# Moving the residual evictions of a graph kernel's prep stage from VectorE to ScalarE

## Chip, cores and metric

One core of a Trainium2 chip. The metric is the device time of one execution in microseconds (us), as the median of several runs. PE is TensorE, PEld its weight loads, DVE is VectorE, ACT is ScalarE, POOL is GpSimd, SP is SyncE.

## The reference

6250 nodes with 256 features each and 200,000 edges sorted by destination. After a layer norm come two graph convolutions with a residual product, then a mixture of six experts of which two are used per node. What matters here, cut down:

```
edge_index = stack([src, dst]); xn = layernorm(x)
deg = segment_sum(ones, dst); dis = rsqrt(deg); norm = dis[src] * dis[dst]
for l in range(2):
    h   = xn @ W[l]
    agg = segment_sum(norm[:, None] * h[src], dst) + b[l]
    xn  = relu(agg + xn @ resW + resb)
x = x + xn
x = x + experts(layernorm(x))          # router, top 2 of 6
```

## The kernel before

Nodes stand in 49 tiles of 128. Layer 1 and layer 2 do not gather: they multiply the 49 tiles of messages (`parts`, a float16 high part and a float16 rest per node) by matrices of edge counts (`counts`), which PE builds from one-hot rows.
The prep stage has these strands:

- **Heads and starts.** The destinations (`dst_sb`) give a histogram of every eighth edge. DVE builds one-hot rows in seven steps (`head_onehots(0)` to `(6)`), PE sums them (`count_heads`), DVE takes them out (`offsets`), PE adds over partitions just ahead of the residual product of tile `OFFSETS_BEFORE`, and DVE makes the start of each node's edges (`starts`).
- **Fetches.** POOL then issues 49 indirect DMAs, one per tile, that read 64 packed edges for each node from DRAM into `windows` (the store `packed_edges` holds source and destination in one 32-bit word, made by `pack`). Ten tiles make a batch. `key_step(n, 0..5)` on DVE waits for batch n and makes its keys and degrees, PE turns them (`turn_keys`), ACT copies them out (`keys_copy`), ACT takes the root of the degrees (`roots`), DVE makes the scale of the messages (`scale`).
- **Residual stage**, one pass over the 49 tiles. DVE takes mean and variance of a group of tiles (`stats(g)`, groups of 4, 4, 4, 6, 6, 6, 6, 6 and 7 tiles). ACT subtracts the mean (`centre`), PE transposes (`turn`), ACT copies out (`turned_copy`), PE multiplies by the residual weights (`residual` of PE, into four banks in turn, so that tile t waits for the eviction of tile t-4), and DVE scales by `rstd`, adds `bias_sum` and writes `res_rows` (`residual` of DVE, L1099). SP stores them in seven pieces.
- **Message stage**, a second pass over the 49 tiles. PE multiplies by the layer's weights (`message`), ACT writes the high part (`high`, L920), DVE the difference (`rest_of`, L1106), ACT converts it (`middle`, L924); tile t waits for the difference of tile t-3. From tile 25 on PE also builds the first pair's edge counts (`count_run`), which ACT evicts (`quad_copy`, L929), from one-hot rows that DVE builds (`pair_heads`, `pair_tiles` at the tiles `ONEHOTS_AFTER_H`).

`norms`, `disorders`, `overflow` and `flag_and_bounds` are bounds and tests that DVE fits in between. The numbers `HIST_BEFORE`, `OFFSETS_BEFORE`, `KEYS_AFTER_RES`, `KEYS_AFTER_H`, `ONEHOTS_AFTER_H` and the tests on `t` in DVE's program are the places of these steps, counted in tiles. After prep, layer 1 (`count_and_sum`) runs over 25 pairs of tiles; `add_res` there adds the residual rows, read back from DRAM into `res_tile`.

Of the kernel before, what the change touches and what calls it, by code (L numbers as in the profile page):

```python
# [18 lines left out]
P = 128  # L19
# [3 lines left out]
I32 = mybir.dt.int32  # L23
ALU = mybir.AluOpType
# [39 lines left out]
class NodeUpdate:  # L64
# [6 lines left out]
    def __init__(self, nc, l, last, sb, sem, shapes, tables, scales, both_w, bias_sum, ident, turn_bank, product_bank, router=None, carve=None):  # L71
# [14 lines left out]
        self.res_back = [sem(f"res_back{l}_{o}") for o in range(2)]  # L86
        self.sum_ready = sem(f"sum_ready{l}")
# [36 lines left out]

    def add_res(self, dve, T, o, u, tile=None):
# [4 lines left out]
        dve.wait_ge(self.res_back[o], u * 16 + 16)  # L130
# [349 lines left out]
def gnn_moe_kernel(nc, x, src, dst, gnn_w, gnn_b, res_w, res_b, router_w1, router_b1, router_w2, router_b2,  # L480
# [35 lines left out]
    with ctx:  # L516
# [152 lines left out]
        BATCH = 10  # L669
# [80 lines left out]
        squares_ready = sem("squares_ready")  # L750
        disorder_ready = sem("disorder_ready")
# [10 lines left out]
        HIST_BEFORE = (None, 1, 2, 3, 4, 5, 6)  # L762
        OFFSETS_BEFORE = 8
        NORMS_BEFORE = 20
        STATS_AFTER = (16, 20, 25, 31)

        KEYS_AFTER_RES = (29, 39)
        KEYS_AFTER_H = (9, 17, 27)
        FLAG_AFTER_H = 33
# [8 lines left out]
        ROOTS = [("rows", g) for g in range(8)] + [("nodes", 0), ("rows", 8)] + [("nodes", n) for n in range(1, batches)]  # L778
# [18 lines left out]
        ONEHOTS_AFTER_H = (6, 14, 16, 24, 27, 30, 33, 36)  # L797
# [4 lines left out]
        with nc.Block() as block:  # L802
# [39 lines left out]
            def _(pool):  # L842
# [11 lines left out]
                nc.gpsimd.tensor_scalar(node_base[:, :], node[:, :], float(P), None, ALU.mult).then_inc(consts_made, 1)  # L854
# [35 lines left out]
            def _(act):  # L890
# [41 lines left out]

                act.wait_ge(cleared, 4)
# [4 lines left out]
                for t in range(tiles):  # L938
# [6 lines left out]
                    turned_copy(t)  # L945
                    if t == 16:
# [3 lines left out]
                    if t == 36:  # L950
                        roots(0)
                    if t == 46:
                        roots(1)
# [3 lines left out]
                for t in range(tiles):  # L957
# [7 lines left out]
                    if t in (9, 17, 27):  # L965
                        roots(2 + (9, 17, 27).index(t))
# [93 lines left out]
            def _(dve):  # L1060
# [31 lines left out]

                def residual(t):
                    if t == GROUPS[group_of(t)][0]:
                        a, b = GROUPS[group_of(t)]
                        dve.wait_ge(roots_ready, ROOTS.index(("rows", group_of(t))) + 1)
                        link(nc.vector.reciprocal(rstd[:, a:b], rstd[:, a:b]))
# [11 lines left out]
                def key_step(n, step):  # L1109
# [18 lines left out]
                    if step == 3:  # L1128
                        link(nc.vector.tensor_scalar(edge_hi[:, :, :], windows[:, ts, :], 14, None, ALU.logical_shift_right))
# [37 lines left out]

                def pack():
                    dve.wait_ge(src_loaded, 16 * 4)
                    link(nc.vector.tensor_scalar(key_i[:, :], dst_sb[:, 0:cols], 14, None, ALU.logical_shift_left))  # L1170
                    nc.vector.tensor_tensor(src_sb[:, :], src_sb[:, :], key_i[:, :], ALU.bitwise_or).then_inc(packed_ready, 1)
                    dve.wait_ge(packed_ready, 1)
# [59 lines left out]
                stats(1)  # L1232
                head_onehots(2)
                head_onehots(3)
                dve.wait_ge(res_w_loaded, 16 * 3)
                for l in range(layers):
                    link(nc.vector.tensor_tensor(bias_sum[:, l, :], bias_sum[:, l, :], res_bias[:, :], ALU.add))
                head_onehots(4)
                residual(0)
                residual(1)  # L1240
                head_onehots(5)
                residual(2)
                pack()
                head_onehots(6)
                residual(3)
                stats(2)
                offsets()
                residual(4)
                residual(5)
                starts()  # L1250
                stats(3)
                for t in range(6, 13):
                    residual(t)
                stats(4)
                for t in range(13, 16):
                    residual(t)
                for t in range(16, tiles):
                    residual(t)
                    if t in STATS_AFTER:
                        stats(5 + STATS_AFTER.index(t))  # L1260
                    if t == 18:
                        disorders()
                    if t == 21:
                        norms()
                    if 24 <= t < 30:
                        key_step(0, t - 24)
                    if 34 <= t < 40:
                        key_step(1, t - 34)
                    if t == 40:
                        scale(0)  # L1270
                scale(1)
                for t in range(tiles):
                    rest_of(t)
                    if t < 6:
                        key_step(2, t)
                    if 8 <= t < 14:
                        key_step(3, t - 8)
# [1487 lines left out]
```

## Time and profile before

| | before |
|---|---|
| median of 3 runs | 1842.45 us (1842.28 to 1843.29) |
| the profiled execution's own time | 1860.24 us |
| its span, first to last instruction | 1857.5 us |
| busy PE, DVE, ACT, POOL | 1779.8, 1036.7, 802.6, 340.4 us |
| mean granted TensorE clock | 0.989 of full speed |

A row of the timeline gives start, duration, engine, line, operation, what it writes and reads, how many instructions it merges, and in brackets the idle time of its engine just before it with what ended that. A row of the table of windows gives, for one stretch, its length, the busy time of PE, PEld, DVE, ACT and POOL with their instructions, then the granted clock as a share of 2.4 GHz, the DMA engines' share and GB/s. A row of the groups of instructions gives busy time, mean ns of one, idle time before them.

### The profile page before, as it was taken

The numbers are of one execution on the slowest core, as the hardware profiler recorded it, in microseconds if no ns is written. First come the engines' busy times: TensorE is split into PE (matmuls) and PEld (weight loads), VectorE is DVE, ScalarE is ACT, GpSimd is POOL, SyncE is SP. The second block draws the span as 40 slices with busy tenths as digits, with TensorE's granted clock in tenths as the row PEclk, the third lists the DMA queues.
The fourth block names the chain that finished last, engine by engine and source line by source line (L and its number), as shares of the span: only waits on it lengthen the run. The fifth ranks groups of instructions, "written<-read, shape, count | busy, mean of one in ns | idle before, by whom it ended". The sixth has DMA issues, their size and how long they took to land. (4 is left out here: it accounts for less than half of the span.)

```text
span 1857.5 us, 41227 instructions
## 1 busy us (share of the span) xinstructions
PE 1779.8 (96%) x14272; PEld 1044.8 (56%) x14272; DVE 1036.7 (56%) x2813; ACT 802.6 (43%) x1822; POOL 340.4 (18%) x345
## 2 busy tenths in 40 slices
PE   4897999999999999999899999999999999899997
PEld 3675444444444444444444444444444478788886
DVE  7885655555555556555324444444444568555554
ACT  2467555555555555555312222222222232565553
POOL 1780000000000000000001111111111123333333
PEclk9999999999999999999999999999999999999999
DMA  7374999999898988899985555555554489323542
GB/s 222 102 133 63 334 291 319 313 319 265 269 299 260 308 249 281 318 359 337 352 318 185 184 184 184 187 186 184 184 184 184 182 261 331 94 88 112 140 135 78
DMA packets 135987, 416.81 MB, mean 224 GB/s; under 512 B 13685, under 2 KB 81611, under 8 KB 129640
## 3 DMA queue, kind: packets, MB, share of 16 engines
q1 hardware_dynamic: 90376, 255.13, 39.9%
q0 software_dynamic: 45392, 160.65, 29.6%
q8 instruction: 36, 0.59, 0.1%
q14 instruction: 39, 0.32, 0.1%
q10 hardware_dynamic: 144, 0.13, 0.0%
HBM read 162.27 MB, written 262.07 MB: 228 GB/s over the span
## 5 line engine op out<-in xcount | busy, mean ns | idle before, releaser
L1475 PE MATMUL bank<-parts,counts 128*128 128x512 f16 x4704 | 1078.9, 380 | 3.3 <-DVE counts L1590 3.3
L1475 PEld LDWEIGHTS bank<-parts,counts 128*128 128x128 f16 x4704 | 442.8, 98 | 509.0 <-issue 28.5
L1634 ACT ACTIVATE counts<-bank 128x392 f16<-128x392 f32 x768 | 336.5, 501 | 296.1 <-PE bank L631 296.1
L640 DVE TENSOR_TENSOR rows<-rows,iota_lo 128x2048 bf16<-128x2048 bf16 (+1 forms) x384 | 322.1, 890 | 20.3 <-PE bank L631 19.3
L631 PEld LDWEIGHTS bank<-rows 64*128 64x128 bf16 x6144 | 95.2, 94 | 82.1 <-issue 78.0
L467 POOL DMA_INDIRECT first_rows<-route_rows,route_spot_i x49 | 47.8, 976 | 498.7 <-DVE tokens L458 394.4
L2265 PE MATMUL bank<-y_t,counts 128*128 128x256 f32 x480 | 115.2, 383 | 5.7 <-ACT y_t L2337 5.1
L631 PE MATMUL bank<-rows 64*128 64x49 bf16 x6144 | 116.8, 185 | 0.1
L2265 PE MATMUL bank<-h_t,counts 128*128 128x256 f32 x480 | 113.7, 380 | 0.0
L2294 PE MATMUL bank<-counts,h_t 128*128 128x256 f32 x480 | 113.5, 380 | 0.0
L1490 ACT ACTIVATE middle<-bank 128x256 f32<-128x256 f32 x98 | 37.3, 381 | 175.9 <-PE bank L1475 161.7
L2479 DVE TENSOR_SCALAR h_t<-bank,counts 128x256 f32<-128x256 f32 x120 | 57.8, 482 | 89.8 <-PE bank L2265 89.8
L2265 PEld LDWEIGHTS bank<-y_t,counts 128*128 128x128 f32 x480 | 92.0, 192 | 19.2 <-issue 6.4
L2341 ACT ACTIVATE h_t<-bank,counts 128x256 f32<-128x256 f32 x120 | 56.1, 468 | 100.5 <-PE bank L2265 88.8
L2294 PEld LDWEIGHTS bank<-counts,h_t 128*128 128x128 f32 x480 | 90.8, 190 | 12.2
L2366 ACT ACTIVATE counts<-parts 128x514 f32 x135 | 92.6, 700 | 9.2 <-issue 2.3
L388 DVE TENSOR_TENSOR route_prob<-bank,router_b_sb 128x12 f32<-128x12 f32 (+1 forms) x25 | 4.3, 170 | 161.6 <-PE bank L378 161.6
L183 PE MATMUL bank<-both_w,rows 128*128 128x512 f32 x196 | 92.2, 593 | 0.0
L2265 PEld LDWEIGHTS bank<-h_t,counts 128*128 128x128 f32 x480 | 86.7, 190 | 9.5
L192 DVE TENSOR_TENSOR res_next<-bank,bias_sum 128x256 f32<-128x256 f32 x49 | 20.8, 425 | 120.8 <-PE bank L183 111.6
L1496 DVE TENSOR_TENSOR sums<-middle,bank 128x256 f32<-128x256 f32 x98 | 41.3, 421 | 82.3 <-ACT middle L1490 81.3
L2570 POOL DMA_INDIRECT first_out<-both_w,to_row x60 | 60.6, 1010 | 129.7 <-DVE both_w L2492 94.2
(275 smaller groups left out, 1759.1 us busy)
## 6 DMA issues: line engine op xcount, KB each, us to landing
counts_table<-counts SPq DMA_DIRECT2D x25, 3136.0 KB, 15.3
counts<-counts_table SPq DMA_DIRECT2D x24, 3136.0 KB, 12.5
first_rows<-zero_rows POOLq DMA_DIRECT2D x3, 10530.0 KB, 59.7
second_rows<-zero_rows POOLq DMA_DIRECT2D x3, 10449.0 KB, 77.0
first_out<-zero_rows POOLq DMA_DIRECT2D x3, 10368.0 KB, 54.9
res_tile<-res_table SPq DMA_DIRECT2D x98, 128.0 KB, 2.8
first_rows<-zero_rows POOLq DMA_DIRECT2D x1, 10270.0 KB, 58.7
second_rows<-zero_rows POOLq DMA_DIRECT2D x1, 10191.0 KB, 68.6
```

What stands on the lines that cost most here:

```text
L183: mm = nc.tensor.matmul(self.product_bank[:, :], self.x1_t[:, o, k * P:(k + 1) * P], self.both_w[:, self.l + 1, k, :], start=k == 0, stop= ...
L467: pool.indirect_dma_start(table, bass.IndirectOffsetOnAxis(ap=self.spot_i[:, b, c, o:o + 1], axis=0), rows[:, b, o, lo:hi], None, bounds_c ...
L631: mm = nc.tensor.matmul(out[:, u * tiles:(u + 1) * tiles], lo[rows, i, :, j], hi[rows, i, :, j], start=True, stop=True)
L640: return nc.vector.tensor_tensor(rows, k, v, ALU.is_equal)
L1475: mm = nc.tensor.matmul(acc[:, 0:2 * dim], counts[:, b, s, o * P:(o + 1) * P], parts[:, s, :], start=s == 0, stop=s == tiles - 1)
L1634: nc.scalar.activation(counts[:, b, :, quad_nodes(q)], bank[4 + q % 4][:, 0:RUN * tiles].rearrange("p (n s) -> p s n", s=tiles), ACT.Copy) ...
L2265: mm = nc.tensor.matmul(to[m][:, 0:ROWS], weights_of(k, n)[:, kf, m * P:(m + 1) * P], source[:, k % 2, kf, :], start=kf == 0, stop=kf == K ...
L2294: mm = nc.tensor.matmul(outs_bank[k % 2][:, cols_of], h2_t[:, k % 2, kf, h * P:(h + 1) * P], weights_of(k, 2)[:, kf, :], start=kf == 0, st ...
L2341: nc.scalar.activation(to[:, k % 2, 0, :], frm[0][:, 0:ROWS], ACT.Relu, bias=bias_of(k, n, 0)).then_inc(low_out, 1)
L2366: nc.scalar.activation(w[:, k % WB, part], held[:, bass.ds(e, 1), part].rearrange("p a n -> p (a n)"), ACT.Copy).then_inc(w_loaded[n][k % ...
L2479: nc.vector.tensor_scalar(to[:, k % 2, 1, :], frm[1][:, 0:ROWS], bias_of(k, n, 1), 0.0, ALU.add, ALU.max).then_inc(high_out, 1)
L2570: pool.indirect_dma_start(table, bass.IndirectOffsetOnAxis(ap=to_row[:, k % SB, h:h + 1], axis=0), result[:, k % 2, cols_of], None, bounds ...
```

## The change

Five edits to the prep stage, and one that follows from them in layer 1.

1. The residual products of tiles 0 to 39 are evicted by ACT, as a copy scaled by `rstd`, inside its loop two tiles behind `turned_copy`; DVE evicts tiles 40 to 48. The reciprocal of a group's `rstd` becomes a step of its own on DVE (`inverse`) with a semaphore (`rstd_ready`).
2. The bias is no longer added there. In layer 1 DVE adds it to `res_tile` (`add_bias`, 49 instructions of 128x256), ahead of `add_res`.
3. `pack` moves from DVE (two instructions) to ACT (one, which writes the destinations into the upper 16 bits of the source words); the destination then stands at bit 16 and not 14, so the shift and `node_base` change.
4. DVE's program of the residual stage is no longer tied to tiles: statistics, one-hots, starts, norms, disorders and the keys of batch 0 follow each other. `starts` comes after the sum ahead of tile 18, not 8.
5. Keys of batch 0 turn at tiles 44 to 48 of the residual stage, those of batches 1 to 4 at tiles 5, 15, 26 and 37 of the message stage (before: batches 0 and 1 in the residual stage, 2 to 4 at 9, 17 and 27). `overflow` goes to tile 39, `flag_and_bounds` from tile 40 to 46.

The paths for irregular graphs only share some semaphores, and this input does not take them.

```diff
-        HIST_BEFORE = (None, 1, 2, 3, 4, 5, 6)
-        OFFSETS_BEFORE = 8
+        HIST_BEFORE = (None, 1, 5, 7, 10, 14, 16)
+        OFFSETS_BEFORE = 18
+        LATE_RES = 40
-        ONEHOTS_AFTER_H = (6, 14, 16, 24, 27, 30, 33, 36)
+        ONEHOTS_AFTER_H = (7, 9, 17, 19, 27, 29, 37, 40)
...
+                def residual(t):
+                    act.wait_ge(products_ready, t + 1)
+                    act.wait_ge(rstd_ready, group_of(t) + 1)
+                    nc.scalar.activation(res_rows[:, t, :], res_bank(t)[:, 0:dim], ACT.Copy, scale=rstd[:, t:t + 1]).then_inc(res_ready, 1)
...
+                def pack():
+                    act.wait_ge(dst_loaded, 16 * 3)
+                    act.wait_ge(src_loaded, 16 * 4)
+                    nc.scalar.activation(src_sb[:, :].bitcast(U16).rearrange("p (c h) -> p c h", h=2)[:, :, 1], dst_sb[:, 0:cols], ACT.Copy).then_inc(packed_ready, 1)
...
+                    if 2 <= t < LATE_RES + 2:
+                        residual(t - 2)
+                    if t == PACK_AT:
+                        pack()
...
+                def inverse(g):
+                    a, b = GROUPS[g]
+                    dve.wait_ge(roots_ready, ROOTS.index(("rows", g)) + 1)
+                    nc.vector.reciprocal(rstd[:, a:b], rstd[:, a:b]).then_inc(rstd_ready, 1)
...
-                    nc.vector.scalar_tensor_tensor(res_rows[:, t, :], res_bank(t)[:, 0:dim], rstd[:, t:t + 1], bias_sum[:, 0, :],
-                                                   ALU.mult, ALU.add).then_inc(res_ready, 1)
+                    dve.wait_ge(res_ready, t)
+                    nc.vector.tensor_scalar(res_rows[:, t, :], res_bank(t)[:, 0:dim], rstd[:, t:t + 1], None, ALU.mult).then_inc(res_ready, 1)
...
+    def add_bias(self, dve, T, o, u):
+
+        dve.wait_ge(self.res_back[o], u * 16 + 16)
+        self.nc.vector.tensor_tensor(self.res_tile[:, o, :], self.res_tile[:, o, :], self.bias_sum[:, 0, :], ALU.add).then_inc(self.res_biased, 1)
...
                 for t in range(tiles):
                     rest_of(t)
+                    n, step = divmod(t - 1, BATCH)
+                    if 0 <= step < 6 and n + 1 < batches:
+                        key_step(n + 1, step)
+                    if t in SCALE_AFTER_H:
+                        scale(1 + SCALE_AFTER_H.index(t))
```

ACT's program in the middle of the residual stage, before. `counts<-counts,row_mean` is `centre`, `counts<-bank` is `turned_copy`:

```order
L893 ACTIVATE counts<-counts,row_mean 128x256
L903 ACTIVATE counts<-bank3 128x256
L893 ACTIVATE counts<-counts,row_mean 128x256
L903 ACTIVATE counts<-bank2 128x256
L893 ACTIVATE counts<-counts,row_mean 128x256
```

The same place now, with `parts<-bank,rstd` the residual's eviction:

```order
L908 ACTIVATE counts<-counts,row_mean 128x256
L918 ACTIVATE counts<-bank3 128x256
L923 ACTIVATE parts<-bank1,rstd 128x256
L908 ACTIVATE counts<-counts,row_mean 128x256
L918 ACTIVATE counts<-bank2 128x256
L923 ACTIVATE parts<-bank6,rstd 128x256
```

Each tile has a third ACTIVATE between the copy and the next `centre`.

DVE's program between `starts` and the middle of the residual stage, before (`parts<-bank,rstd,bias_sum` is its eviction of a residual):

```order
L1166 CAST start_i<-start 128x50
L1084 BN_STATS row_stats<-counts 128x6 x6
L1086 TENSOR_TENSOR row_sum<-row_stats 128x6
L1087 TENSOR_TENSOR row_gap<-row_stats 128x6
L1088 TENSOR_TENSOR row_var<-row_stats 128x6
L1089 TENSOR_SCALAR row_mean<-row_sum 128x6
L1090 TENSOR_TENSOR row_gap<-row_gap 128x6
L1091 SCALAR_TENSOR_TENSOR row_var<-row_gap,row_var 128x6
L1099 SCALAR_TENSOR_TENSOR parts<-bank,rstd,bias_sum 128x256 x2
L1097 RECIPROCAL rstd<-rstd 128x4
L1099 SCALAR_TENSOR_TENSOR parts<-bank,rstd,bias_sum 128x256 x4
```

and the end of that stretch now, from the last statistics on:

```order
L1123 RECIPROCAL rstd<-rstd 128x7
L1148 TENSOR_SCALAR key_i<-onehot_lo 128x640
L1149 TENSOR_SCALAR edge_hi<-onehot_lo 128x640
L1153 TENSOR_TENSOR node_keys<-edge_hi,node_base 128x640
L1155 CAST node_keys<-key_i 128x640
L1158 TENSOR_SCALAR edge_hi<-onehot_lo 128x640
L1160 TENSOR_TENSOR key_i<-edge_hi,node 128x640
L1162 COPY over<-key_i 128x10
L1163 TENSOR_REDUCE deg<-key_i 128x10
L1129 TENSOR_SCALAR parts<-bank,rstd 128x256 x3
```

No eviction of a residual stands on DVE ahead of the keys of batch 0; the first is that of tile 40.

DVE's program at the end of prep, now; `rest<-bank,message_scale,parts` is `rest_of`:

```order
L1135 SCALAR_TENSOR_TENSOR rest<-bank,message_scale,parts 128x256 x5
L1221 TENSOR_REDUCE over<-bank 128x1
L1222 TENSOR_SCALAR over<-over 128x1
L1223 CAST flag<-over 128x1
...
L1230 TENSOR_SCALAR dis_next<-dis,power 128x49
L1232 TENSOR_SCALAR dis_back<-dis,power 128x49 x2
L1135 SCALAR_TENSOR_TENSOR rest<-bank,message_scale,parts 128x256 x2
```

`flag_and_bounds` stands ahead of the last two differences; before, eight followed it.

## Rows read from the trace of the kernel before

**Rows 1.** Windows of the stages: residual, message with two halves, layer 1.

```profile
50.00:111.50 61.50, 53.19 (x259) 42.41 (x260) 51.68 (x156) 34.92 (x95) 47.05 (x47) 0.94 0.39 114
111.50:143.00 31.50, 29.63 (x161) 21.72 (x159) 30.09 (x62) 22.16 (x62) 29.24 (x43) 1.00 0.94 136
143.00:157.50 14.50, 10.59 (x130) 7.85 (x123) 9.12 (x18) 11.98 (x34) 0.00 (x0) 1.00 1.02 134
...
162.60:185.30 22.70, 16.44 (x182) 11.48 (x181) 14.00 (x39) 18.09 (x49) 0.00 (x0) 1.00 0.01 2
185.30:840.00 654.70, 654.63 (x7950) 323.24 (x7951) 387.07 (x607) 360.76 (x909) 37.43 (x11) 1.00 0.94 297
```

**Rows 2.** Groups of DVE's instructions, from 0 to 185 us.

```profile
L1099 DVE SCALAR_TENSOR_TENSOR parts<-bank,rstd,bias_sum 128x256 f32<-128x256 f32 x49 | 22.7, 481 | 8.8 <-PE bank L991 8.2
...
L1131 DVE TENSOR_TENSOR key_i<-edge_hi,node 128x640 f32<-128x640 int32 x5 | 4.1, 820 | 0.0
```

**Rows 3.** PE's timeline in the residual stage.

```profile
67.98 3.60 PE L1040 MATMUL bank<-parts,ones 128*128 128x512 f32 x8
...
72.50 1.03 PE L991 MATMUL bank<-both_w,counts 128*128 128x256 f32 x4
...
73.58 1.03 PE L991 MATMUL bank<-both_w,counts 128*128 128x256 f32 x4
...
80.62 1.86 PE L991 MATMUL bank<-both_w,counts 128*128 128x256 f32 x4 [2.54 <-DVE parts L1099]
...
111.47 9.01 PE L1002 MATMUL bank<-both_w,counts 128*128 128x256 f32 x40
```

**Rows 4.** DVE's timeline up to the starts and behind them.

```profile
21.04 2.02 DVE L640 TENSOR_TENSOR onehot_lo<-head_lo,iota_lo 128x3584 bf16<-128x3584 bf16 x1
...
23.76 2.02 DVE L640 TENSOR_TENSOR onehot_lo<-head_lo,iota_lo 128x3584 bf16<-128x3584 bf16 x1
...
49.22 0.19 DVE L1166 CAST start_i<-start 128x50 int32<-128x50 f32 x1
49.32 2.05 DVE L1084 BATCH_NORM_STATS2 row_stats<-counts 128x6 f32<-128x256 f32 x6
...
52.12 0.87 DVE L1099 SCALAR_TENSOR_TENSOR parts<-bank,rstd,bias_sum 128x256 f32<-128x256 f32 x2
```

**Rows 5.** POOL's timeline, first and last of the 49 fetches.

```profile
50.44 1.21 POOL L876 DMA_INDIRECT onehot_lo<-packed_edges,start_i  x1 [42.03 <-POOLq L873]
...
113.76 0.98 POOL L876 DMA_INDIRECT onehot_lo<-packed_edges,start_i  x1 [0.30 <-issue]
```

**Rows 6.** Groups of ACT's instructions, from 0 to 185 us.

```profile
L893 ACT ACTIVATE counts<-counts,row_mean 128x256 f32<-128x256 f32 x49 | 24.4, 501 | 32.2 <-DVE row_mean L1089 32.2
L920 ACT ACTIVATE parts<-bank,message_scale 128x256 f16<-128x256 f32 x49 | 23.0, 469 | 2.7 <-DVE message_scale L1141 2.2 <-PE bank L1002 0.4
...
L903 ACT ACTIVATE counts<-bank 128x256 f32<-128x256 f32 x49 | 18.5, 378 | 24.5 <-PE bank L983 24.4
...
L907 ACT ACTIVATE keys_t<-bank 128x256 bf16<-128x256 f32 x25 | 9.6, 384 | 4.8 <-PE bank L1012 4.8
...
L949 ACT ACTIVATE parts<-both_w 128x2048 f32<-128x2048 f32 x1 | 1.9, 1898 | 0.0
```

**Rows 7.** DVE's timeline in the message stage: tiles 0, 24, the bounds, tile 48.

```profile
113.04 0.48 DVE L1106 SCALAR_TENSOR_TENSOR rest<-bank,message_scale,parts 128x256 f32<-128x256 f32 x1 [0.50 <-ACT parts L920]
...
142.73 0.48 DVE L1106 SCALAR_TENSOR_TENSOR rest<-bank,message_scale,parts 128x256 f32<-128x256 f32 x1
...
173.19 0.15 DVE L1198 TENSOR_REDUCE over<-bank 128x1 f32<-128x3 f32 x1
...
176.76 0.88 DVE L1106 SCALAR_TENSOR_TENSOR rest<-bank,message_scale,parts 128x256 f32<-128x256 f32 x2
...
183.05 0.48 DVE L1106 SCALAR_TENSOR_TENSOR rest<-bank,message_scale,parts 128x256 f32<-128x256 f32 x1 [0.19 <-ACT parts L920]
```

**Rows 8.** PE's timeline, its longest idle time in the message stage.

```profile
159.18 1.75 PE L1002 MATMUL bank<-both_w,counts 128*128 128x256 f32 x4 [3.46 <-issue]
```

More of the change, by code:

```diff
@@ L23 @@
 I32 = mybir.dt.int32
+U16 = mybir.dt.uint16
 ALU = mybir.AluOpType
@@ L86, in __init__ @@
         self.res_back = [sem(f"res_back{l}_{o}") for o in range(2)]
+        self.res_biased = None if last else sem(f"res_biased{l}")
         self.sum_ready = sem(f"sum_ready{l}")
@@ L129, in add_res @@
         dve.wait_ge(self.sums_out, T + 1)
-        dve.wait_ge(self.res_back[o], u * 16 + 16)
+        if self.last:
+            dve.wait_ge(self.res_back[o], u * 16 + 16)
+        else:
+            dve.wait_ge(self.res_biased, T + 1)
         if later:
@@ L775, in keys_after_h @@
             return next(((n + len(KEYS_AFTER_RES)) * BATCH // 2 + t - a for n, a in enumerate(KEYS_AFTER_H) if a <= t < a + BATCH // 2), None)
-        ROOTS = [("rows", g) for g in range(8)] + [("nodes", 0), ("rows", 8)] + [("nodes", n) for n in range(1, batches)]
+        ROOTS = [("rows", g) for g in range(9)] + [("nodes", n) for n in range(batches)]
         def res_bank(t):
@@ L964, in _ @@
                         middle(t - 1)
-                    if t in (9, 17, 27):
-                        roots(2 + (9, 17, 27).index(t))
+                    if t in ROOTS_AFTER_H:
+                        roots(1 + ROOTS_AFTER_H.index(t))
                 middle(tiles - 1)
@@ L1232, in _ @@
                 stats(1)
+                inverse(0)
                 head_onehots(2)
                 head_onehots(3)
+                stats(2)
+                inverse(1)
+                head_onehots(4)
+                stats(3)
+                inverse(2)
+                head_onehots(5)
+                head_onehots(6)
+                inverse(3)
+                stats(4)
+                offsets()
+                stats(5)
+                inverse(4)
+                starts()
                 dve.wait_ge(res_w_loaded, 16 * 3)
@@ L1237, in _ @@
                     link(nc.vector.tensor_tensor(bias_sum[:, l, :], bias_sum[:, l, :], res_bias[:, :], ALU.add))
[L1238 to L1251, printed above, removed]
@@ L1252, in _ @@
-                for t in range(6, 13):
-                    residual(t)
[L1254 to L1270, printed above, removed]
@@ L1271, in _ @@
-                scale(1)
+                stats(6)
+                inverse(5)
+                stats(7)
+                inverse(6)
+                norms()
+                stats(8)
+                inverse(7)
+                disorders()
+                inverse(8)
+                for step in range(6):
+                    key_step(0, step)
+                residual(LATE_RES)
+                residual(LATE_RES + 1)
+                residual(LATE_RES + 2)
+                scale(0)
+                for t in range(LATE_RES + 3, tiles):
+                    residual(t)
@@ L1339, in _ @@
                 def _(act):
-                    act.wait_ge(degree_ready, 1)
-                    nc.scalar.activation(true_dis[:, :], degree[:, :], ACT.Sqrt, bias=1.0).then_inc(root_ready, 1)
+                    act.wait_ge(stage_done, DEGREES_MADE)
+                    nc.scalar.activation(true_dis[:, :], degree[:, :], ACT.Sqrt, bias=1.0).then_inc(stage_done, 1)
                 @block.vector
```

85 lines of the change are left out of this document (37 added, 48 removed).

## Prediction, on record before the changed kernel ran

> **What bounds the kernel now.** I read the table of windows first. Layer 1, the 654.7 us behind prep, has PE busy in 654.63 of them [rows 1]: a us that prep gives up moves the end of the kernel by a us, and nothing in layer 1 waits for anything else. So the question is only when prep ends, now at 185.3 us. The windows then split prep. In the residual stage, 50 to 111.5 us, PE is busy in 53.19 of 61.5 us and DVE in 51.68; neither is full. In the first half of the message stage DVE is busy in 30.09 of 31.5 us and bounds it. In the second half ACT is the fullest: 11.98 of 14.5 and 18.09 of 22.7 us [rows 1].
>
> The timeline of PE says why the residual stage is slow. Where nothing disturbs it, one tile starts 1.08 us after the other (72.50, 73.58) [rows 3]; 49 tiles would be 53 us. But DVE holds statistics, norms, key steps and evictions in one program, and PE waits for an eviction, 2.54 us in the row shown, after which the same four products take 1.86 us, not 1.03 [rows 3]: the clock had fallen from 2.4 towards 1.2 GHz while it stood, and 0.94 of full is the stage's mean [rows 1]. The stage begins early, but before the starts are made at 49.22 [rows 4] only 10 of the 49 tiles are through. Fetches run from 50.44 to 113.76 on POOL, 1.3 us apart [rows 5]; the message stage begins at 111.47 [rows 3], when the last batch is just being fetched, so a message stage that begins earlier needs key steps that come later in it.
>
> **The change, part by part.**
>
> *Start of the stage.* Up to 21.04 us DVE does what it did [rows 4]. Then come five more head one-hots at 2.72 us (23.76 less 21.04), statistics of one group of 4 (about 2.1 us, scaled from 2.80 for six tiles, 52.12 less 49.32) and one of 6 [rows 4], and four reciprocals, estimated at 0.2: the fourth reciprocal, for which ACT's eviction of tile 12 waits, is due at 21.04 + 13.6 + 4.9 + 0.8 = 40.3. Removed from this stretch are the two instructions of pack and six evictions. From there PE has tiles 14 to 17 to do (4.4 us), two head sums (about 1 us each), and ACT the squares of the weights (1.90 us, unchanged) [rows 6]: the sum ahead of tile 18 comes at 48.5, and the starts at 50.1, against 49.3. So the fetches are 0.9 us later, and PE stands at tile 18 where it stood at 10.
>
> *Pack on ACT.* No row has it. 1568 elements lie between 256 (0.38 us) and 2048 (1.90 us) [rows 6]; I take 1.5. It stands where ACT then waits for the statistics of group 2, due near 28, so it costs nothing; without that cover, 1.5.
>
> *Evictions on ACT.* The nearest row is L920, the same bank read with a per-partition scale: 469 ns, against 481 on DVE [rows 2, 6]. ACT's instructions overlap by about 0.1 us, so a tile costs centre 0.40, copy 0.28, eviction 0.37 to 0.40: 1.05 to 1.08, no more than PE's 1.08 [rows 3, 6]. I take PE's pace, 1.09 a tile, with the end of range 1.3 where the two loops lock. The Trainium skill, page "ScalarE: Activation LUTs", section "Rules for kernel authors", says to use VectorE and not ScalarE for mul and add, with up to about 3x per element. The rows have the two level for float32 out of PSUM (469 against 481), so the sum does not go by it; what it would do is a rival below.
>
> *Rest of the residual stage.* Tiles 18 to 21 end at 48.5 + 4.4 = 52.9. The norm products take 3.6 [rows 3]: 56.4. Then 27 tiles at 1.09, five turns of keys at 0.25: 87.1. DVE has 2.8 us of statistics against 6.5 us of PE per group and stays ahead, but reciprocals now wait for ACT's roots, and the keys of batch 0 (eight instructions, one of which takes 0.82 us [rows 2]; 4.6 us estimated, at most 6.6) follow the last of them, due near 77: eviction 40 comes near 82, just when PE's tile 44 needs its bank. I add 0.9. Messages begin at 88, not 111.47, and the first difference at 89.8, not 113.04 [rows 3, 7]: 23.2 us gained. The fetches of batch 0 are in by about 66 and hide.
>
> *First half of the message stage.* DVE bound it: 29.7 us from tile 0 to 24 [rows 7]. It had three batches of keys and three and a half one-hot steps; it now has nearly two and a half batches and four steps. I take 29.7 (28 to 31): tile 24 at 119.5. Batches 1, 2, 3 are wanted near 91, 103, 115 and are in by about 80, 93, 106; batch 4 is wanted at tile 31, near 131, its last fetch is issued at 114.6 [rows 5].
>
> *Second half.* 40.3 us from tile 24 to 48 [rows 7]. ACT, the fullest engine, gets ten copies of keys in it, not five. One is 0.38 us [rows 6], between 0.3 and 0.9 with the turn it waits for; at 0.5, 2.5 us. Key steps of batch 4 on DVE lie between differences: 0 to 4, I take 1. The bounds (173.19 to 176.76, 3.6 us) [rows 7] stood at tile 40, where PE and ACT could use some of it; at tile 46 only two high parts can hide them. 0 to 3.6 more, I take 1.6. PE stood 3.46 us with nothing that the profile shows before 159.18 [rows 8], while the DMA engines were full (1.02 share) [rows 1]. POOL's copies of the expert weights follow the fetches at the same time as now, and so fall wholly on this half; 0 to twice 3.5 us of it may come, I take half of what is there, 1.7 less. Sum: 40.3 + 2.5 + 1 + 1.6 - 1.7 = 43.7, so tile 48 at 163.2, against 183.05: 19.9 us earlier.
>
> *Layer 1.* 49 additions of about 0.43 us on DVE, which is busy in 387 of 655 us [rows 1]: 21 us of idle time used. The first waits for `res_tile` and holds DVE's one-hot rows behind it: 0.5 us. If the cover were gone in each of 24 pairs, up to 10 us; PE's idle time there is nil now, and DVE runs ahead by a step, so I take 0. Semaphores added cost nothing beside that.
>
> Together 19.9 - 0.5 = 19.4 us. Of the profiled execution, 1860.2 us with a span of 1857.5, 1841 would be left. Runs without the profile take 1842.45, 18 us less; I take off the same 19.4 and get **1823.0**. 0.2% (3.7 us) is about what a measurement can tell from no change.
>
> **Rivals.**
>
> *The loops lock* (0.18). ACT has three instructions a tile, each waiting on another engine, at 1.05 to 1.08 against PE's 1.08. At 1.25 a tile, 31 tiles are 5 us longer, and a second stop of PE like that at 159 adds 3.5: 1827 to 1834. For it: ACT was never above 0.6 busy in that stage [rows 1]. Against it: it is two tiles behind, with four banks.
>
> *The message stage gives back less* (0.13). No stop of PE, bounds and key steps hidden: 43.7 becomes 37 to 39, and 1817 to 1812.
>
> *ScalarE three times slower at this* (0.02). An eviction of 1.4 us makes a tile 2.1; 22 tiles from 18 to 39 are 22 us longer and the early ones 8: 1853. L920 speaks against it [rows 6]. This is where the rule of the Trainium skill's page "ScalarE: Activation LUTs" would lead.
>
> *Slower: PE at 1.2 GHz through the residual stage* (0.03). Before, the clock fell when PE had waited [rows 3]. If ACT feeds it in drops, a tile takes twice 1.08, and from 18 such tiles on the 19.4 us are gone; all 31 from tile 18 add 33 and give 1856. Against it: at 0.86 busy the clock was 0.94 of full [rows 1], and fewer waits should follow.
>
> *Nothing gained* (0.02): the bias additions take PE's cover in layer 1 and locked loops the rest; 1842.
>
> **How the numbers follow.** Forecast 0.62, 1823 with its own 1817 to 1828. The locked and the short case reach to 1834 and 1812; leaving out the outer edge of each, the range is 1813 to 1832. Faster: 0.62 + 0.18 + 0.13 = 0.93. Same 0.02. Slower 0.02 + 0.03 = 0.05.
>
> **What the changed profile would show.** Starts near 50; evictions by ACT near 470 ns; PE's residual tiles 1.09 apart from 56 on, at full clock; messages from 88; difference of tile 24 near 119.5 and of tile 48 near 163; first product of layer 1 near 165.5; layer 1 with PE full. Wrong would be: tiles 1.2 or more apart with PE waiting for ACT, DVE waiting for a fetch, or idle PE in layer 1 behind one-hot rows.

## The result, and the profile after

The changed kernel takes 1829.31 us (median of 4 runs, 1827.04 to 1832.29); the kernel before, on the same chip, 1842.87 us (4 runs, 1842.28 to 1846.48). The ratio is 0.991, 95% interval 0.9887 to 0.9932: about 13.5 us faster, where 19.4 were forecast. The two profiled executions stand further apart (1860.24 and 1832.29 us, spans 1857.5 and 1829.7); most of what prep does not explain of that lies at the border of layers 1 and 2, and is taken up under "Where the rest went".

The windows of the changed kernel, with the columns of [rows 1] (length, then busy time of PE, PE's weight loads, DVE, ACT and POOL, granted clock, DMA share, GB/s), cut where its stages begin:

```profile
50.00:88.00 38.00, 37.51 (x199) 30.77 (x198) 27.12 (x84) 30.01 (x88) 27.71 (x28) 1.00 0.41 121
...
111.50:143.00 31.50, 26.54 (x275) 18.74 (x273) 24.72 (x50) 24.88 (x70) 30.28 (x44) 1.00 0.76 99
143.00:157.50 14.50, 6.88 (x67) 5.14 (x66) 3.91 (x10) 5.64 (x16) 1.01 (x2) 0.69 1.03 140
157.50:170.40 12.90, 6.36 (x52) 4.07 (x51) 6.66 (x27) 6.98 (x20) 0.00 (x0) 0.76 0.31 56
170.40:812.00 641.60, 641.57 (x7771) 316.12 (x7772) 394.29 (x637) 352.47 (x888) 37.43 (x11) 1.00 0.94 305
```

The residual stage is 38 us long in place of 61.5 [rows 1], with PE busy in 37.51 of them at full clock. The part from 143 to 157.5 is the bad one: PE 6.88 us busy in 14.5, at 0.69 of its clock, with every compute engine idle more than it works and the DMA engines full. Layer 1 has PE full, as before.

PE's timeline of the changed kernel (start, duration, engine, line, operation, and in brackets the idle time before it and what ended it), which answers to [rows 3, 8]:

```profile
53.45 3.60 PE L1067 MATMUL bank<-parts,ones 128*128 128x512 f32 x8
...
72.06 1.03 PE L1018 MATMUL bank<-both_w,counts 128*128 128x256 f32 x4
...
73.14 1.03 PE L1018 MATMUL bank<-both_w,counts 128*128 128x256 f32 x4
...
81.39 1.10 PE L1018 MATMUL bank<-both_w,counts 128*128 128x256 f32 x4 [0.49 <-DVE parts L1129]
...
87.64 2.54 PE L1029 MATMUL bank<-both_w,counts 128*128 128x256 f32 x11
...
153.37 1.44 PE L1029 MATMUL bank<-both_w,counts 128*128 128x256 f32 x3 [6.68 <-issue]
...
170.43 5.30 PE L1489 MATMUL bank<-parts,counts 128*128 128x512 f16 x12 [6.28 <-DVE counts L1604]
```

Residual tiles start 1.08 us apart, and from 50 us on PE's only wait in that stage is 0.49 us, for DVE's eviction of a late tile. Messages begin at 87.64 (111.47 before). The next thing that stands out is 6.68 us before 153.37 that nothing in the profile ends: "issue" means that the engine waited for no semaphore that the trace shows. In what follows such an idle time is called PE's stop. Before, such a stop was 3.46 us long [rows 8].

DVE's timeline and groups of the changed kernel, against [rows 4, 7]:

```profile
50.79 0.19 DVE L1195 CAST start_i<-start 128x50 int32<-128x50 f32 x1
...
89.22 0.48 DVE L1135 SCALAR_TENSOR_TENSOR rest<-bank,message_scale,parts 128x256 f32<-128x256 f32 x1 [1.10 <-ACT parts L940]
...
118.30 0.48 DVE L1135 SCALAR_TENSOR_TENSOR rest<-bank,message_scale,parts 128x256 f32<-128x256 f32 x1
...
156.71 0.48 DVE L1135 SCALAR_TENSOR_TENSOR rest<-bank,message_scale,parts 128x256 f32<-128x256 f32 x1 [7.58 <-ACT parts L940]
...
164.22 0.15 DVE L1221 TENSOR_REDUCE over<-bank 128x1 f32<-128x3 f32 x1
...
167.78 0.88 DVE L1135 SCALAR_TENSOR_TENSOR rest<-bank,message_scale,parts 128x256 f32<-128x256 f32 x2
170.08 0.29 DVE L1604 TENSOR_TENSOR counts<-counts,ident_h 128x256 f16<-128x256 f16 x1 [1.43 <-PEq L817]
```

Tile 0's difference is at 89.22, tile 24's at 118.30: 29.1 us for the first half, 29.7 before. From tile 24 to tile 48 (the second of the two at 167.78) it is 49.9 us, where 40.3 were taken before and 43.7 were forecast. The bounds stand from 164.22 to 167.78. The groups of ACT's instructions up to 170 us (count, then busy time and mean ns) show its new work:

```profile
L940 ACT ACTIVATE parts<-bank,message_scale 128x256 f16<-128x256 f32 x49 | 23.1, 471 | 1.5 <-PE bank L1029 1.2
...
L923 ACT ACTIVATE parts<-bank,rstd 128x256 f32<-128x256 f32 x40 | 19.1, 477 | 0.8 <-DVE rstd L1123 0.8
...
L956 ACT ACTIVATE src_sb<-dst_sb 128x1568 uint16<-128x1568 int32 x1 | 2.0, 2006 | 0.0
```

### The profile page after: what moved, and what is told of

Same layout as the page of the kernel before. It is cut to its first block and busy times, and to the rows that moved or that the text cites. A ratio compares the mean times of both kernels' runs of the same rounds, so it can differ in the third digit from the quotient of the medians.

```text
span 1829.7 us, 41310 instructions
## 1 busy us (share of the span) xinstructions
PE 1769.5 (97%) x14272; PEld 1041.2 (57%) x14272; DVE 1034.7 (57%) x2820; ACT 817.5 (45%) x1863; POOL 341.2 (19%) x345
## 3 DMA queue, kind: packets, MB, share of 16 engines
q1 hardware_dynamic: 90376, 255.13, 40.3%
q0 software_dynamic: 45392, 160.65, 29.1%
```

## Experiments

Each kernel was timed in five rounds beside the kernel before. There were three groups; the kernels of one group ran on one chip, and one is compared with another only inside its group. In all of them the ratio is to the kernel before.

### First group: what holds the second half back

**The changed kernel with the copies of the expert weights in layer 1.** POOL's copies (`router_w...`, `expert_pack`), issued behind the fetches until 143.5 us, are moved to the head of `store_zeros`, ahead of the zero stores:

```diff
                 for t in range(tiles):
                     pool.indirect_dma_start(windows[:, t, :], ...)
-                pool.dma_start(router_w1_sb[:, :, :], ...)
-                for e in range(experts): ...
...
         def store_zeros(pool):
+            pool.dma_start(router_w1_sb[:, :, :], ...)
+            for e in range(experts): ...
```

> The changed kernel with POOL's copies of the router and expert weights moved out of prep, to the head of POOL's program in layer 1. Theory (PE's program load waits behind full DMA engines): the one stop of 6.7 us at 146.7 is gone, with the slow clock behind it some 8 to 10 us of prep; prep ends near 161 and the time falls from 1829 to 1819 to 1822, with less spread between runs. Rival (the stop belongs to PE's own program at that place, whatever the DMA engines do): a stop of several us stays and the time stays at 1827 to 1832. Second rival (the copies only move): the zero stores end about 30 us later and layer 2's first scatters wait, which gives part back.

Measured: 1847.75 us, ratio 1.0007 (0.9993 to 1.0021). In its trace the stop is gone and prep ends early. PE's and DVE's timeline:

```profile
160.56 0.88 DVE L1124 SCALAR_TENSOR_TENSOR rest<-bank,message_scale,parts 128x256 f32<-128x256 f32 x2
```

```profile
163.21 5.29 PE L1478 MATMUL bank<-parts,counts 128*128 128x512 f16 x12 [6.28 <-DVE counts L1606]
```

and its window, with no DMA traffic to speak of where the changed kernel had a share of 1.03:

```profile
145.00:150.00 5.00, 4.06 (x44) 3.10 (x45) 2.39 (x5) 3.44 (x11) 0.00 (x0) 0.79 0.01 3
```

Tile 24 is at 118.11 here and tile 48 at 161.0: 42.9 us without a stop, against 49.9 with one of 6.68. So the stop is nearly the whole difference, and it comes with the full DMA engines. (The granted clock falls here too, to 0.79 in the row shown, although PE did not stop.) But the 7.2 us that prep gives up are more than lost. Layer 1 is 7.9 us longer (163.21 to 909.86, against 170.43 to 909.15), and layer 2 with what follows 15.2 us (935.7 against 920.5). The zero stores start behind the copies, and the last is issued at 901.95 in place of 844.62. This is the second rival of the expectation; the 1819 to 1822 us of its theory were missed, though the stop went as it said.

**The same move in the kernel before.** 

> The kernel before with the same move of the copies. Theory: its stop of 3.5 us at 155.7 is gone, with the slow clock 4 to 5 us; 1837 to 1839. The difference between this kernel and the changed one with the same move is then what the change is worth without stops: 17 to 20 us. Rival: nothing changes, 1842, and the difference is the same 13.5 us as between the two originals.

Measured: 1869.07 us, ratio 1.0132 (1.0112 to 1.0151). Prep ends 5.7 us earlier (its first product of layer 1 at 179.6), and the kernel is 23 us slower. Both the 1837 to 1839 us of the theory and the 1842 of its rival were missed: in both kernels, moving the copies into layer 1 costs more than it gives.

**The flag and the bounds at tile 43 in place of 46.**

```diff
-                    if t == 46:
+                    if t == 43:
                         flag_and_bounds()
```

> The changed kernel with the bounds and the flag at tile 43 of the message stage, not 46. Theory (at 46 only two tiles are left to hide 3.6 us, and the profile shows ScalarE idle 3.2 us there): 1.5 to 3 us less, 1826.5 to 1828. Rival (PE then waits for the differences of tiles 44 and 45 as it did before at tile 40, and the place is worth nothing): within 0.5 us of 1829.

Measured: 1831.34 us, ratio 0.9918 (0.9902 to 0.9934): no gain. The trace says why, and it was not among the expectations. ACT's last instruction of prep, then DVE's first of layer 1, then PE's stop of the message stage and its first product:

```profile
163.75 0.42 ACT L944 ACTIVATE parts<-rest 128x256 f16<-128x256 f32 x1 [0.24 <-DVE rest L1135]
```

```profile
169.76 0.29 DVE L1604 TENSOR_TENSOR counts<-counts,ident_h 128x256 f16<-128x256 f16 x1 [6.05 <-PEq L817]
```

```profile
149.38 0.81 PE L1029 MATMUL bank<-both_w,counts 128*128 128x256 f32 x3 [2.02 <-issue]
...
170.11 4.81 PE L1489 MATMUL bank<-parts,counts 128*128 128x512 f16 x12 [7.42 <-DVE counts L1604]
```

The chain of messages was done at 164.2, 4.9 us before the changed kernel's (168.30 + 0.81 = 169.1 for ACT's last instruction), mostly because the stop was 4.7 us shorter in this execution; yet layer 1 began at the same time. Its windows of the last us of prep:

```profile
163.00:164.00 1.00, 0.00 (x0) 0.00 (x0) 0.48 (x1) 0.76 (x3) 0.00 (x0) 0.50 0.27 74
164.00:165.00 1.00, 0.00 (x0) 0.00 (x0) 0.00 (x0) 0.16 (x1) 0.00 (x0) 0.50 0.08 17
165.00:166.00 1.00, 0.00 (x0) 0.00 (x0) 0.00 (x0) 0.00 (x0) 0.00 (x0) 0.50 0.00 0
```

No compute engine works from 164.2 to 169.8; the DMA engines move the last bytes of the copies until just before 165. The new theory was that POOL's part of prep does not end before the copies are through, some 5 us after their last byte, and that this is a **floor** under the end of prep, near 169.5, just where the chain of messages ended too. Before, the copies ended near 163, but prep ended at 185, and the floor was out of sight.

**The evictions on ACT alone**, in the kernel before: its order of DVE's steps and its packing stay, the evictions of 40 residual tiles move to ACT and the bias into layer 1.

```diff
                     turned_copy(t)
+                    if 2 <= t < LATE_RES + 2:
+                        residual(t - 2)
...
+                        if there(i * 2 - 3):
+                            if r == 0:
+                                update.add_bias(dve, i * 2 - 3, 1, i - 2)
```

> The kernel before with only the evictions of tiles 0 to 39 on ScalarE and the bias added in layer 1; VectorE keeps its order with its steps tied to tiles, and the starts stay ahead of tile 8. Theory (the eviction is what tied PE to VectorE, but the order must follow, since VectorE now runs ahead into steps that wait for fetches while a reciprocal stands behind them): messages begin near 95 to 100 and key batches 2 to 4, wanted at tiles 0, 8 and 18, wait for their fetches until 118; prep ends 8 to 14 us earlier than before, 1829 to 1835. Rival (the eviction alone carries it, the order is worth nothing): 1827 to 1830, messages near 88. Second rival (the order carries it): 1840 to 1843.

Measured: 1835.83 us, ratio 0.9942 (0.9926 to 0.9958). In its trace messages begin at 103.26, 8.2 us earlier than before, and the first product of layer 1 comes at 179.24, although PE's stop is longer (4.95 us). The expectation had messages at 95 to 100 and 1829 to 1835 us; both were missed, by 3.3 and 0.8 us. So the evictions alone bring 8.2 of the 23.8 us by which messages begin earlier, and 6.1 of the 14.9 at prep's end; of the time, 0.58% of about 0.9%. The rest is put down, by difference, to the new order of DVE's steps and the packing, which stand on the freed DVE; no kernel has the new order alone. Note that 6.1 us of prep stand beside 9.9 us of time here (1845.71 less 1835.83): the time does not follow prep's end us for us.

### Second group: the copies earlier, and the bias

> The changed kernel itself, unchanged, as the reference on this chip for the others of this group. Both theories: 1829 us within 3, ratio 0.991.

Measured: 1849.75 us (1846.8 to 1853.06), ratio 0.9912 (0.9883 to 0.9941). This chip is about 1% slower in every kernel, and noisier. Its trace shows the floor in the changed kernel itself, and plainer than any other. ACT's last instruction of prep, DVE's first of layer 1 and PE's first product:

```profile
165.49 0.81 ACT L944 ACTIVATE parts<-rest 128x256 f16<-128x256 f32 x2 [3.17 <-DVE rest L1135]
```

```profile
172.30 0.29 DVE L1604 TENSOR_TENSOR counts<-counts,ident_h 128x256 f16<-128x256 f16 x1 [6.45 <-PEq L817]
```

```profile
172.65 5.04 PE L1489 MATMUL bank<-parts,counts 128*128 128x512 f16 x12 [11.31 <-DVE counts L1604]
```

PE's stop was only 3.11 us and the chain ended at 166.3, 2.8 us before that of the first execution, yet layer 1 began 2.2 us later than there (172.30 against 170.08). The copies ran until 167.5 here.

**Two of six experts copied ahead of the fetches**, in the time in which POOL waits for the starts:

```diff
+                pool.wait_ge(gnn_w_loaded, 16 * 3)
+                pool.dma_start(router_w1_sb[:, :, :], ...)
+                for e in range(2): ...
                 pool.wait_ge(packed_stored, 16)
                 pool.wait_ge(starts_ready, 1)
                 for t in range(tiles):
                     pool.indirect_dma_start(windows[:, t, :], ...)
-                for e in range(experts): ...
+                for e in range(2, experts): ...
```

> The changed kernel with the router's tables and two of the six experts' weights copied before GpSimd's fetches (issued from about 41 us, when the weights have landed, until about 50) in place of behind them; the other four stay behind the fetches, issued until about 133 us. Nothing is left out and nothing more lies in layer 1. Theory (the copies of six experts, which fill the DMA engines until 164 us, cost the preparation its end twice: TensorE's stop of 6.7 us at 147 and GpSimd's part of the preparation, which is not over before about 169): the DMA engines are free of copies by about 150, TensorE's stop shrinks or goes, the first product of layer 1 stands near 163.5 as it did with the copies in layer 1, and since layer 1 has no copies to carry, this gain stays: 1829.3 - 7 = 1822 us, ratio 0.987. Rival (the total is set by what layers 1 and 2 do with the transfers, not by when the preparation ends): no change, 1829. A second rival: the two early experts slow the packed edge list or the first fetches, the key batches come late, and the time is 1829 to 1833.

> The same with the flag and the bounds at tile 43 in place of 46. Theory: with the copies over early, the end of the preparation follows the chain of DVE and ScalarE again, so the 4 to 5 us by which this edit alone brought that chain forward (ScalarE done at 164.2 in place of 169.1) now count in part: the first layer-1 product at 159 to 161, 1818 to 1821 us, 2 to 4 below the kernel without it. Rival (something other than the copies held the end at 169.8 when the flag stood at 43): no difference to the kernel with early copies alone.

Measured: 1848.68 us (1840.6 to 1850.4), ratio 0.9881 (0.9849 to 0.9912), and with the flag at 43 1845.62 us (1840.55 to 1847.8), ratio 0.9887 (0.9854 to 0.992). The intervals overlap those of the changed kernel, so the times settle nothing here; the 1822 and 1818 to 1821 us of the theories were missed on a chip that is slower throughout, and so was the ratio of 0.987. The first products of layer 1 do bear on the floor. With the copies early alone, then with the flag at 43 too:

```profile
168.98 5.04 PE L1498 MATMUL bank<-parts,counts 128*128 128x512 f16 x12 [6.30 <-DVE counts L1613]
```

```profile
163.80 5.10 PE L1498 MATMUL bank<-parts,counts 128*128 128x512 f16 x12 [2.81 <-DVE counts L1613]
```

With the copies behind the fetches, a chain of messages that was done 4.9 us earlier moved this product by 0.3 us (170.43 to 170.11). With the copies over by about 151, the product comes 3.7 us before that of the changed kernel on this chip (168.98 against 172.65), and it follows the chain again: the flag at 43 moves it by 5.2 us, of which 3.1 are a shorter stop of PE (1.29 us) and at most 2.1 the edit. Both products came later than expected (163.5, and 159 to 161). The first expectation was wrong about the stop: it did not go but came earlier, 4.34 us before 137.98, still under full DMA engines:

```profile
137.98 0.28 PE L641 MATMUL bank<-src_sb,onehot_hi 64*128 64x49 bf16 x5 [4.34 <-issue]
```

**The bias left out.** 

> The changed kernel without the 49 additions of the bias to the residual rows of layer 1: this part of the computation is left out, everything else is as in the changed kernel. The prediction's term was 0 (plus 0.5 us for the first one): 1829 us within 1, since TensorE is full in layer 1. Rival (DVE's additions lie on the path of some tiles): 49 times 0.42 us, or some of it, is saved, down to 1809 us.

Measured: 1851.03 us (1845.63 to 1862.95), ratio 0.9926 (0.9897 to 0.9956), against 0.9912 with the additions. They cost nothing that can be seen on this noisy chip; the rival's 20 us are excluded.

### Third group: pack, and three experts early

> The changed kernel once more, unchanged: on this chip the reference for the two others of this group. Ratio 0.991, as in both groups before.

Measured: 1830.76 us (1827.51 to 1834.22), ratio 0.9918 (0.99 to 0.9935). Here PE's stop was 4.32 us and the chain ended at 166.7; layer 1 still began at the floor:

```profile
165.33 0.88 DVE L1135 SCALAR_TENSOR_TENSOR rest<-bank,message_scale,parts 128x256 f32<-128x256 f32 x2
169.44 0.29 DVE L1604 TENSOR_TENSOR counts<-counts,ident_h 128x256 f16<-128x256 f16 x1 [3.23 <-PEq L817]
```

**Pack back on DVE**, ahead of its third group of statistics:

```diff
                 head_onehots(3)
+                pack()
                 stats(2)
```

> The changed kernel with the packing of the keys back on VectorE (two instructions over 1568 columns, 0.97 and 1.79 us in the kernel before) ahead of its third statistics group, and off ScalarE (2.01 us). My theory: the starts come about 2.8 us later (53.6 in place of 50.8), fetches and key batches with them, and the messages still begin at 87.6 because the residual tiles on TensorE, 1.08 apart, set that; but GpSimd's copies end 2.8 us later too, so the floor that they put under the end of the preparation goes from about 170 to 172.5 in the profile: plus 0 to 2.5 us on the time. Rival (the preparation ends by the chain of messages alone and the copies are no floor): 0. Rival two (VectorE's delay reaches ScalarE's evictions by the reciprocals, TensorE waits, and everything moves by 2.8): plus 2.8 or more.

Measured: 1833.49 us (1831.77 to 1833.87), ratio 0.9932 (0.9915 to 0.9949), 2.7 us above the control with ranges that overlap. Its trace shows what the second rival said of the start of the messages, against my theory. Messages, PE's stop and the first product of layer 1:

```profile
91.10 1.25 PE L1027 MATMUL bank<-both_w,counts 128*128 128x256 f32 x5
...
157.37 1.44 PE L1027 MATMUL bank<-both_w,counts 128*128 128x256 f32 x3 [7.22 <-issue]
...
174.78 4.15 PE L1494 MATMUL bank<-parts,counts 128*128 128x512 f16 x12 [6.29 <-DVE counts L1609]
```

The starts came at 54.25 (51.12 in the control), and messages at 91.10 (87.97): both moved by 3.1 us, about the length of VectorE's two instructions. DVE's stretch up to the starts bounds the residual stage after all. The end of prep is 5.0 us later (174.78 against 169.79), but that is not pack's alone: the stop was 2.9 us longer in this execution, and the copies ran until 169.3 (164.7 in the control), so the floor stood near 174 too, and the trace does not tell which of the two held layer 1. Of the time, the 2.7 us are not clear of noise.

**Three experts ahead of the fetches, flag at 43.** The edit is that of the second group with `range(3)`.

> Three of the six experts' weights copied before the fetches in place of two, with the flag and the bounds at tile 43. Theory: the first fetch is issued at about 55, which the key batches' slack of about 10 us absorbs; the copies are over by about 143, before TensorE's loads of instructions at 146 to 150, so that TensorE's stop without a releaser stays under 1 us; the first product of layer 1 at 160 to 162 in the profile, 8 to 10 before the changed kernel. If no bound stands behind it, the time falls by as much, to a ratio of 0.986. Rival (the zero stores of layer 1, twelve transfers one after the other in GpSimd's queue, end the gain at the border of layers 1 and 2, where TensorE waits about 10 us for the parts while one of them is still under way): half of the gain or less stays, ratio 0.988 to 0.990. Second rival (fetches late): a wait for keys in the message stage, ratio over 0.991.

Measured: 1825.45 us (4 runs, 1824.38 to 1828.23), ratio 0.9893 (0.9872 to 0.9914), 5.3 us below the control of the same chip. No stop of PE is left in the message stage, and prep ends at 161.7:

```profile
150.33 0.39 PE L641 MATMUL bank<-src_sb,onehot_hi 64*128 64x49 bf16 x16 [0.32 <-DVE src_sb L650]
...
161.73 5.06 PE L1498 MATMUL bank<-parts,counts 128*128 128x512 f16 x12 [2.82 <-DVE counts L1613]
```

```profile
140.00:145.00 5.00, 3.42 (x30) 2.01 (x28) 3.16 (x7) 4.00 (x13) 0.00 (x0) 1.00 0.28 63
145.00:150.00 5.00, 4.39 (x48) 3.17 (x48) 2.56 (x6) 3.71 (x11) 0.00 (x0) 1.00 0.01 3
```

The copies are over by 143. Prep is 8.1 us shorter than the control's (169.79), of which 5.3 show in the time. It is the fastest version of this study by its median; the two ranges just overlap (1828.23 and 1827.51), and the edit moves copies and flag at once, so the time does not say what each is worth. The theory was right about the stop and prep's end (160 to 162) and missed the ratio of 0.986; the 0.988 to 0.990 of its first rival came, but nothing here shows that the zero stores took the rest: the wait at the border of layers 1 and 2 is 1.02 us in this trace.

## Why the prediction held, and where its size was off

**The bound** was read rightly in the main: prep's end moved by 14.9 us in the profiles (185.31 to 170.43), the time by 13.5. "A us that prep gives up moves the end of the kernel by a us" is too exact, though. With the evictions alone 6.1 us of prep stand beside 9.9 of time, with three experts early 8.1 beside 5.3, and with the copies in layer 1 prep gave 7.2 us and the time nothing.

**Start of the stage.** Starts at 50.79 (50.1 forecast), fetches from 52.0. Right within 0.7 us. That pack on ACT costs nothing fits too, though it takes 2.01 us, not 1.5: ACT still waits 1.09 us for DVE's next mean behind it. Put back on DVE it makes the starts and the messages 3.1 us later.

**The clock before.** One reading was wrong without harm to the sum: the prediction has the clock fall while PE stood ahead of 80.62. The granted clock was 1.00 up to that point and 0.50 from 81.0 to 84, when PE worked again.

**Evictions on ACT.** 477 ns each (469 forecast from L920), tiles 1.08 us apart (1.09 forecast), clock 1.00. The loops did not lock. The Trainium skill, page "ScalarE: Activation LUTs", section "Rules for kernel authors", would rather have this multiplication on VectorE; its figure of up to about 3x per element is given for bf16. Here DVE's remaining nine evictions take 483 ns each and ACT's forty 477. In this trace, float32 out of PSUM has no such advantage.

**Rest of the residual stage and first half.** Messages at 87.64 (88), first difference 89.22 (89.8), tile 24 at 118.30 (119.5). The forecast was 1.2 us late there.

**Second half: the step that failed.** The sum had 43.7 us; it took 49.9. Without the stop of PE the sum reads 42.0 (43.7 less the 1.7 left for it), and the kernel without a stop took 42.9. So the keys on ACT, the late key steps and the bounds at tile 46 were sized within a us taken together; no run separates them. The term "PE stood 3.46 us [...] I take half of what is there, 1.7 less" is the one that was mis-sized: it leaves a stop of 1.8 us, and the stop was 6.68 us in the profiled execution, 4.32 and 3.11 in two other executions of the same kernel. The half took 49.9, 47.1 and 47.4 us in these three, against 42.9 without a stop, so a stop can cost more than its length. It follows the copies, and the copies now fall wholly on this half; the prediction said so and still credited a smaller stop. Its own bounds reached to twice 3.5 us, which covers it. But the forecast's own case ended at 1828, and the range reached 1832 only by the locked loops, which did not happen: that it held is in part luck.

**Behind the second half** stands a limit which the prediction did not have at all: POOL's copies. In the control the chain would have let layer 1 begin 1.8 us earlier (1.0 us after ACT's last instruction at 166.65, as in the changed kernel, not 2.8), in the kernel with the flag at 43 4.6 us and in the changed kernel on the slower chip 5.0 us earlier; a shorter chain gains nothing there. So the mis-sized stop is not all of the miss: with a stop as short as forecast, layer 1 could still not have begun near 165.5, since in these three executions the floor stood at 169.4 to 172.3.

**Layer 1.** PE full, bias additions at nothing: right, also by the kernel without them.

**The rivals.** "The loops lock" had the wrong mechanism, but its second half, a stop of PE longer than before, is what came, and its time (1827 to 1834) is what was measured; the forecast's own 1817 to 1828 was missed by 1.3 us. The other four did not happen. One of them was also added up wrongly: 43.7 becoming 37 to 39 makes 1816 to 1818, not "1817 to 1812".

**Where the rest went.** The profiled executions differ by 27.8 us, not by 13.5. The 13 us above prep's share are mostly at the border of layers 1 and 2 (the wait there is 9.1 us shorter, and the product after it is at full clock, 3.18 in place of 5.45 us). Twelve zero stores run one after the other through layer 1; the last is issued at 844.62 in the changed kernel, at 882.22 in the kernel before and at 879.31 in the changed kernel on the slower chip. PE's first product of layer 2 in these three, in that order:

```profile
909.15 3.18 PE L1821 MATMUL bank<-parts,counts 128*128 128x512 f16 x14 [1.02 <-DVE sums L1510]
```

```profile
932.95 5.45 PE L1802 MATMUL bank<-parts,counts 128*128 128x512 f16 x14 [10.14 <-DMA parts<-parts_table]
```

```profile
923.77 5.37 PE L1821 MATMUL bank<-parts,counts 128*128 128x512 f16 x14 [9.93 <-DMA parts<-parts_table]
```

So it is in all thirteen traces: where the last zero store was issued by 853 us (six traces) the wait is 1.02 us, where it was issued at 874 or later (seven) 3.5 to 10.5. The prediction took the profiled execution of before as a constant 18 us above the others; part of those 18 may be this wait. That the late store is its cause fits, but no kernel was made that changes it alone.

**Open.** What PE waits for in its stops. One packet of the instruction queue q8 lies inside each stop of 3 us or more, in eight traces: from 148 to 151 us in the changed kernel (its DMA view shows queue, kind, packets, MB, share), from 156 to 158 in the kernel before, from 134 to 136 with two experts early. In the ninth, the stop of 2.02 us with the flag at 43, the packet passes about 1 us before the stop begins. Such packets pass without a stop as well, in the changed kernel at 130 and 161 us. In five executions with the copies where the changed kernel has them (that kernel three times, the flag at 43, no bias) the stop begins behind the same product, at 146.7 to 147.4.

```profile
q0 software_dynamic: 221, 0.53, 103.1%
q8 instruction: 1, 0.02, 2.7%
```

The stops vanish when the copies are elsewhere (copies in layer 1, or three experts early) and move to 138 when the copies' load moves. That they do not come without the copies' load is shown; that PE is out of instructions behind the copies' packets is the reading that fits, and is argued. The Trainium skill, page "DMA: Bandwidth & Descriptors", section "Queues, rings and completion order", has each DMA engine go round its queues packet by packet; by that, one packet would wait for one packet of the copies, and no run here shows when it was asked for. What the profile counts as a packet of the copies took 0.22 us on the mean in these 3 us (1.031 of 16 engines' 3 us, over 221 packets), so one of those alone would not fill a stop of 6.68 us. That layer 1 does not begin until about 5 us after the copies' last byte is read from four traces in which the chain was done earlier: 4.9 us with the flag at 43 (164.9 to 169.76), 4.7 in the control (164.7 to 169.44), 4.8 in the changed kernel on the slower chip (167.5 to 172.30) and 4.9 without the bias (166.3 to 171.22). That it is POOL that waits, and what it does in these 5 us, is not shown.

## What to carry to other kernels

When a stage is made shorter, look at every queue that runs beside it, not only at the engines that bound it: here transfers that had some 17 us of slack at the end of prep (185 against a floor near 168, an estimate from copies that were over by 163) became its floor, and 4.9 us off the bounding chain were worth 0.3 us until they were moved. A stall "by nothing that the profile shows" under full DMA engines varies from one execution to the next (3.11 to 6.68 us here in one kernel); size it by the worst case and try moving the transfers away from it. Idle time of a queue ahead of its real work (POOL from 8 to 52 us) is a place to try for transfers that nobody waits for. And a difference between two profiled executions (27.8 us) is not the gain (13.5): a wait that one of them has elsewhere is not to be counted.

## What the runs showed of the hardware

PE stood up to 7.22 us, with the DMA engines full, for something other than a semaphore that the profile shows, and the same kernel shows 3.11, 4.32 and 6.68 us for it in three executions. Behind such a stop it ran at 1.2 GHz: in the control it stopped from 147.0 to 151.3, and the granted clock was 0.50 from 149.5 to 156. A stage whose POOL program issued copies did not end until 4.7 to 4.9 us after their last byte, in four traces, with all compute engines idle for up to 6 us. ACT converts 1568 int32 to every second uint16 in 2.01 us, where DVE took 0.97 and 1.79 us for a shift and an or.
